# Three attentions whose score products use half the rows of the array, two heads side by side, and whose ends are rearranged

## The chip, the cores and the metric

The kernel runs on one core of a Trainium2 chip. Its time is the device time of one launch in microseconds (us). Lower is better. TensorE (PE) multiplies matrices, VectorE (DVE) and ScalarE (ACT) work on tiles and read what PE leaves in PSUM, GpSimd (POOL) works on tiles in SBUF, and SyncE (SP) issues most of the transfers. The launch works through eight batches, one pass of a loop for each, and ends with a recurrent part over all eight.

## The reference

A residual stream x of 8 batches, 512 tokens and 128 features goes through four layers. Each normalises x, takes an attention (or a memory) of the normalised rows and a feed-forward gate of them, and adds their product:

```python
xn = _layernorm(x, axis=-1)
s = _L1_attn_ref(xn, L1_attn_Wq, L1_attn_Wk, L1_attn_Wv, L1_attn_Wo)
g = _silu(_L1_ffn_ref(xn, L1_ffn_w_gate, L1_ffn_w_up, L1_ffn_w_down))
x = x + s * g
```

The attentions of the first three layers have 16 heads of 8 dimensions. The first sees all 512 keys; the other two are causal and have an output projection. All is fp32. The change touches these three attentions, and of the first layer also the end of its gate, a ternary feed-forward under a silu.

## The kernel before

Each pass of the loop holds, in order: the first attention (below: the full one), with the hidden layers of the ternary feed-forward beside it; the normalisation and projections of the second layer and its causal attention (the second), with a feed-forward and late experts beside it; a local attention; the third layer's causal attention (the third), with a gated unit and projections beside it; a second local attention, the last feed-forward and the experts.

Queries and keys are fp32. They are split into three bf16 parts each, high, middle and low, stored in DRAM and spread from there (`spread_loads`) so that rows of the contraction are pairs of a query part and a key part: 3 by 3 pairs of 8 dimensions are the 72 rows of a bf16 product. `qs` and `ks` hold 16 heads side by side in those rows, with two more rows for the maximum.

One attention works in four groups of four heads, on a grid of steps, eight to a group. `first_scores` makes queries by keys in PSUM banks 0 and 1 (line 440); in the causal attentions another product, of the identity and a mask of -1e30, adds the mask to the diagonal block (line 446). DVE reduces each bank to the negative maximum of its rows (line 618), and the product of score item n waits until item n-2 is reduced. When a group is through, PE transposes its maxima (line 468), ACT and DVE split them into two bf16 parts, and SP writes these as rows 72 and 73 of `qs` (line 566). Twelve steps after its first item, `second_scores` makes keys by queries with the 74 rows (line 458), so that the maximum is already taken off; ACT takes the exponential (line 538) from a ring of three banks; GpSimd clears above the diagonal in the causal attentions; and every second step four products of 32 columns side by side weigh the values (line 501). At a group's end the sums come back by a transpose (line 474) and DVE divides.

A full attention has 16 items of one head and one tile of queries in a group. A causal one has 11: one item with four heads for the first tile, two with two heads for the second tile, and one for each head of the others. Work of the feed-forward is called in between by step numbers (`yield`). `keep_busy` adds products that nobody reads (line 96): in the second attention they stand between the score products of the last steps. At the end of the second and third attention PE transposes `att`, ACT copies it (line 552), PE projects it (line 516), and DVE copies the result from PSUM before it goes on (line 631).

Of the kernel before, what the change touches and what calls it, by code (L numbers as in the profile page):

```python
# [26 lines left out]
E3, H3 = 8, 256  # L27
BELOW = 1.0 - 2.0 ** -22
# [291 lines left out]

def spread_loads(nc, K, engine, queries=True, keys=True):

    engine.wait_ge(K.saved, 32)
    for g in range(NG):
        heads = slice(4 * g, 4 * g + 4)
        part = lambda m: K.parts_d[m].rearrange("i (d h) t -> i d h t", d=HD)[:, :, heads, :]
        if keys:
            engine.dma_start(K.ks[72:74, heads, :], K.ones_d[:, heads, :]).then_inc(K.spread[g], 16)
        for i in range(3):
            rows = slice(24 * i, 24 * i + 24)  # L330
            if queries:
                engine.dma_start(K.qs[rows, heads, :],
                                 part(0)[i].unsqueeze(0).to_broadcast([3, HD, 4, T])).then_inc(K.spread[g], 16)
            if keys:
                engine.dma_start(K.ks[rows, heads, :], part(1)).then_inc(K.spread[g], 16)


class Beside:
# [10 lines left out]
    FILLED = {}  # L349
    started = False  # L350
# [19 lines left out]
def attention(nc, K, causal, wo=None, bo=None, combine=True, beside=None, after_store=False,  # L370
# [9 lines left out]
    QUADS, LAG, KR = 3, 12, 74  # L380
# [36 lines left out]
    with ExitStack() as tmp:  # L417
# [5 lines left out]
        with nc.Block() as block:  # L423
            @block.tensor
            def _(pe):
# [6 lines left out]
                def first_scores(n):  # L432
                    g, (t, heads) = n // PER, items[n % PER]
                    b, keys = n % 2, (t + 1) * P if causal else T
                    if n % PER == 0:
                        pe.wait_ge(K.spread[g], 7 * 16)
                    if n >= 2:
                        pe.wait_ge(reduced, n - 1)
                    for i, j in enumerate(heads):
                        mm = nc.tensor.matmul(K.ps[:, b, i * keys:(i + 1) * keys],  # L440
                                              K.qs[0:72, 4 * g + j, t * P:(t + 1) * P], K.ks[0:72, 4 * g + j, 0:keys],
                                              start=(i == 0), stop=not causal)
# [8 lines left out]
                def second_scores(m):  # L451
                    g, (k, j) = m // 16, divmod(m % 16, 4)
                    h, b = 4 * g + j, bank("second", m)
                    if m % 16 == 0:
                        pe.wait_ge(rows, 32 * (g + 1))
# [2620 lines left out]
```

## Time and profile before

| | |
|---|---|
| median of three runs | 4192.31 us (4190.34 to 4197.16) |
| the profiled execution | 4196.52 us, span 4193.1 us |
| PE busy | 3506.4 us, 84% |
| DVE busy | 2530.1 us, 60% |
| ACT busy | 1823.9 us, 43% |
| mean granted TensorE clock | 0.939 |

The span is the time from the first to the last instruction of the profiled execution. A share of busy time is an average over all stages. Matmuls are pipelined, so a product's row shows more time than it holds the array: what it costs in a stream is the distance between the starts of two rows.

### The profile page before, as it was taken

How to read it: one execution, taken by the hardware profiler on the slowest of the kernel's cores; microseconds unless marked ns; L12 is line 12 of the kernel's file. 1: busy time of each engine (PE TensorE's matmuls, PEld its weight loads, DVE VectorE, ACT ScalarE, POOL GpSimd, SP SyncE). 2: the span in 40 equal slices, each digit the busy share in tenths (PEclk: the TensorE clock that was granted, in tenths of full speed). 3: DMA queues.
4: the chain of work that ended last, by engine and by line, in shares of the span. 5: the costliest groups of instructions: out<-in, count | busy, mean ns of one | idle time of the engine just before them, and what ended most of it. 6: DMA issues, size and time to landing. Idle time of an engine off the chain costs nothing. (4 is left out here: it accounts for less than half of the span.)

```text
span 4193.1 us, 55509 instructions
## 1 busy us (share of the span) xinstructions
PE 3506.4 (84%) x19466; PEld 1814.7 (43%) x19615; DVE 2530.1 (60%) x5500; ACT 1823.9 (43%) x3753; POOL 821.5 (20%) x721
## 2 busy tenths in 40 slices
PE   3988798888988889887988889888898879888867
PEld 1444444444344444454444443444434544444434
DVE  3566655666556655666556665566556665566655
ACT  1544444444443535444444444444354444444414
POOL 1023300331012400233003310124002230033114
PEclk9999999999999999999999999999999999999978
DMA  4000111001011010000111010110200001110130
GB/s 155 25 17 26 36 30 34 31 4 61 5 34 34 1 65 25 17 26 32 34 34 31 4 63 4 34 34 1 65 28 14 27 36 30 34 31 4 63 84 21
DMA packets 87847, 140.06 MB, mean 33 GB/s; under 512 B 12472, under 2 KB 62466, under 8 KB 85002
## 3 DMA queue, kind: packets, MB, share of 16 engines
q1 hardware_dynamic: 81042, 127.30, 9.5%
q10 hardware_dynamic: 6522, 9.06, 0.7%
q8 instruction: 169, 2.77, 0.3%
q14 instruction: 114, 0.93, 0.1%
HBM read 106.14 MB, written 29.39 MB: 32 GB/s over the span
## 5 line engine op out<-in xcount | busy, mean ns | idle before, releaser
L618 DVE TENSOR_REDUCE nmax<-banks 128x1 f32<-128x512 f32 (+3 forms) x1216 | 761.1, 658 | 392.5 <-PE banks L440 228.2
L538 ACT ACTIVATE probs<-banks 128x512 f32<-128x512 f32 (+3 forms) x1024 | 475.7, 526 | 302.9 <-PE banks L458 299.9
L440 PE MATMUL banks<-ks,qs 72*128 72x512 bf16 (+3 forms) x1536 | 464.1, 348 | 98.3 <-DVE nmax L618 68.3
L458 PE MATMUL banks<-qs,ks 74*128 74x512 bf16 (+3 forms) x1536 | 461.9, 338 | 41.2 <-ACT probs L538 17.2
L96 PE MATMUL banks<-filler,identb 128*128 128x512 bf16 x1576 | 427.9, 392 | 36.0 <-PEq L76 26.5
L440 PEld LDWEIGHTS banks<-ks,qs 72*128 72x128 bf16 x1536 | 144.0, 101 | 418.4 <-DVE nmax L618 246.2
L538 ACT ACTIVATE early<-banks 128x256 f32<-128x256 f32 (+3 forms) x512 | 198.1, 440 | 196.6 <-PE banks L458 196.6
L1295 ACT ACTIVATE probs<-banks,nm 128x192 f32<-128x192 f32 x512 | 172.6, 422 | 229.9 <-DVE nm L1247 229.9
L501 PE MATMUL banks<-probs,v 128*32 128x512 f32 (+3 forms) x2048 | 239.1, 539 | 32.4 <-POOL probs L584 22.9
L253 POOL TENSOR_TENSOR rstd<-var,neghalf 128x4 f32<-128x4 f32 (+1 forms) x16 | 21.2, 1324 | 1246.2 <-DVE var L204 1137.8
L96 PEld LDWEIGHTS banks<-filler,identb 128*128 128x128 bf16 x1712 | 171.5, 101 | 205.0 <-issue 63.5
L458 PEld LDWEIGHTS banks<-qs,ks 74*128 74x128 bf16 x1536 | 142.1, 100 | 234.6 <-ACT probs L538 79.0
L1329 POOL TENSOR_TENSOR probs<-probs,inv 128x768 f32<-128x768 f32 x128 | 187.1, 1467 | 259.7 <-DVE inv L1257 259.7
L603 DVE RECIPROCAL rden<-banks 128x16 f32<-128x16 f32 x96 | 24.4, 254 | 317.9 <-PE banks L474 317.0
L446 PE MATMUL banks<-mask_q,identb 128*128 128x128 bf16 (+2 forms) x704 | 186.2, 265 | 0.0
L1199 PE MATMUL banks<-ident,probs 128*128 128x128 f32 x896 | 141.5, 295 | 49.9 <-POOL probs L1329 32.5
L1254 DVE TENSOR_REDUCE total<-probs 128x4 f32<-128x768 f32 x128 | 122.0, 953 | 84.6 <-ACT probs L1295 80.4
L584 POOL TENSOR_SCALAR_AFFINE_SELECT probs<-probs 128x512 f32<-128x512 f32 x128 | 97.3, 760 | 382.4 <-ACT probs L538 382.4
L584 POOL TENSOR_SCALAR_AFFINE_SELECT early<-early 128x512 f32<-128x512 f32 x128 | 92.8, 725 | 397.8 <-ACT early L538 397.8
L1247 DVE TENSOR_REDUCE nm<-banks 128x4 f32<-128x768 f32 x128 | 119.9, 937 | 64.1 <-PE banks L1180 63.9
L1990 PE MATMUL banks<-xnT,w_up_s 128*128 128x512 f32 x320 | 150.6, 609 | 1.4
L1199 PEld LDWEIGHTS banks<-ident,probs 128*128 128x128 f32 x896 | 101.2, 147 | 89.6 <-POOL probs L1329 47.4
(453 smaller groups left out, 6528.2 us busy)
## 6 DMA issues: line engine op xcount, KB each, us to landing
qs<-parts_scratch SPq DMA_DIRECT2D x300, 96.0 KB
ks<-parts_scratch SPq DMA_DIRECT2D x288, 96.0 KB
parts_scratch<-parts SPq DMA_DIRECT2D x50, 384.0 KB, 2.5
shared<-in_w_h SPq DMA_DIRECT2D x17, 1024.0 KB, 7.6
shared<-in_w SPq DMA_DIRECT2D x25, 256.0 KB, 4.0
qs<-max_parts SPq DMA_DIRECT2D x192, 4.0 KB
xn<-in_x SPq DMA_DIRECT2D x9, 256.0 KB, 2.7
factor_scratch<-g SPq DMA_DIRECT2D x9, 256.0 KB, 2.2
```

The source lines that it names most:

```text
L96: nc.tensor.matmul(K.ps[:, bank, :], K.identb[:, :], K.filler[:, :], start=True, stop=True)
L440: mm = nc.tensor.matmul(K.ps[:, b, i * keys:(i + 1) * keys], K.qs[0:72, 4 * g + j, t * P:(t + 1) * P], K.ks[0:72, 4 * g + j, 0:keys], star ...
L446: mm = nc.tensor.matmul(diagonal, K.identb[:, :], K.mask_q[:, :].unsqueeze(1).to_broadcast([P, n_heads, P]), start=False, stop=True)
L458: nc.tensor.matmul(K.ps[:, b, q0:T], K.ks[0:KR, h, k * P:(k + 1) * P], K.qs[0:KR, h, q0:T], start=True, stop=True).then_inc(scored2, 1)
L501: mm = nc.tensor.matmul(K.ps[32 * j:32 * j + 32, 5, q0:T], K.v32[:, k, 4 * g + j, :], probs[:, 4 * (q % QUADS) + j, q0:T], start=(k == 0), ...
L538: nc.scalar.activation(probs[:, 4 * (q % QUADS) + m % 4, q0:T], K.ps[:, bank("second", m), q0:T], ACT.Exp, scale=scale).then_inc(exped, 1)
L584: nc.gpsimd.affine_select(diagonal, diagonal, [[0, 4], [1, P]], ALU.is_ge, 0.0, base=0, channel_multiplier=-1).then_inc(masked, 1)
L618: nc.vector.tensor_reduce(nmax[:, t, h:h + len(heads)], K.ps[:, n % 2, 0:len(heads) * keys].rearrange("p (j k) -> p j k", k=keys), AX.X, A ...
L1199: mm = nc.tensor.transpose(K.ps[:, 4 + e, o:o + P], probs[:, w % RING, e, i, (k - t + 1) * P:(k - t + 2) * P], K.ident[:, :])
L1295: a = nc.scalar.activation(probs[:, w % RING, e, i, 64:256], K.ps[:, 2 * u + e, 256 * i + 64:256 * i + 256], ACT.Exp, bias=nm[:, u, e, i:i ...
L1329: nc.gpsimd.tensor_tensor(x, x, inv[:, w % 2, :, :].rearrange("p e t -> p (e t)").unsqueeze(2).to_broadcast([P, 4, SPAN]), ALU.mult).then_ ...
L1990: mm = nc.tensor.matmul(K.ps[:, 2 * (n % 2) + m, :], K.w3_up[:, e, (2 * m + c) * P:(2 * m + c + 1) * P], K.xnT[:, :], start=True, stop=True)
```

## The change

Seven pairs of parts are left of the nine (the products of the middle and the low part of the keys with the low part of the queries are left out): 56 rows, and with the maximum's two 58. These fit in half of the array's rows. Heads 0 and 1 of a group lie in partitions 0 to 63 of `qs` and `ks`, heads 2 and 3 in partitions 64 to 127, and every score product names its half by `tile_position`. The mask product, the transposes, the weighing and the extra products are made as before. In the full attention the items alternate between the halves (heads 0, 2 for each tile, then 1, 3), and the second products take the heads in the order 2, 0, 3, 1. A causal group has 12 items: the first tile's item of four heads becomes two of two.

Each group's spread is issued for each half apart: 14 transfers for 7, and the rows of the maximum 4 for 2. The silu of the first layer's gate becomes an exponential on ACT and an addition, a reciprocal and a product on DVE, at step 38 (it was at the end), and the output products of that feed-forward start at step 32 (was 36). In the second attention ACT copies the transposed `att` before the gate's silu (was after). The copy of line 631 goes: DVE reads the projection from PSUM in the operation that follows.

```diff
@@ spread_loads
-        heads = slice(4 * g, 4 * g + 4)
-            engine.dma_start(K.ks[72:74, heads, :], K.ones_d[:, heads, :]).then_inc(K.spread[g], 16)
-        for i in range(3):
-            rows = slice(24 * i, 24 * i + 24)
+        for e in range(2):
+            heads = slice(4 * g + 2 * e, 4 * g + 2 * e + 2)
+            for i, n in enumerate((3, 3, 1)):
+                rows = half_rows(2 * e, HD * n, 24 * i)
...
@@ attention
-        items = [(0, (0, 1, 2, 3)), (1, (0, 1)), (1, (2, 3))] + [(t, (j,)) for t in (2, 3) for j in range(4)]
-        by_step = (0, 1, 2, 3, 5, 6, 8, 9, 11)
+        items = [(t, pair) for t in (0, 1) for pair in ((0, 1), (2, 3))] + [(t, (j,)) for t in (2, 3) for j in (0, 2, 1, 3)]
+        by_step = (0, 2, 3, 4, 6, 7, 9, 10, 12)
     else:
-        items = [(t, (j,)) for j in range(4) for t in range(NT)]
+        items = [(t, (j,)) for pair in ((0, 2), (1, 3)) for t in range(NT) for j in pair]
...
+    HEADS, ROWS = (2, 0, 3, 1), 4 * 16
@@ first_scores
-                                              K.qs[0:72, 4 * g + j, t * P:(t + 1) * P], K.ks[0:72, 4 * g + j, 0:keys],
-                                              start=(i == 0), stop=not causal)
+                                              K.qs[rows, slot, t * P:(t + 1) * P], K.ks[rows, slot, 0:keys],
+                                              start=(i == 0), stop=not causal, tile_position=(64 * (j // 2), 0))
@@ second_scores
-                    nc.tensor.matmul(K.ps[:, b, q0:T], K.ks[0:KR, h, k * P:(k + 1) * P], K.qs[0:KR, h, q0:T],
-                                     start=True, stop=True).then_inc(scored2, 1)
+                    nc.tensor.matmul(K.ps[:, b, q0:T], K.ks[half_rows(j, KR), slot, k * P:(k + 1) * P],
+                                     K.qs[half_rows(j, KR), slot, q0:T], start=True, stop=True,
+                                     tile_position=(64 * (j // 2), 0)).then_inc(scored2, 1)
@@ sync
-                    for i in range(2):
-                        sp.dma_start(K.qs[72 + i:73 + i, 4 * g:4 * g + 4, :], mparts[:, g % 2, i, :]).then_inc(rows, 16)
+                    for e in range(2):
+                        for i in range(2):
+                            sp.dma_start(K.qs[half_rows(2 * e, 1, SCORE_ROWS + i), 2 * g:2 * g + 2, :],
+                                         mparts[2 * e:2 * e + 2, g % 2, i, :]).then_inc(rows, 16)
@@ the ends
+                o = K.att[:, :, :]
-                    ch.do(nc.vector.tensor_copy(K.att[:, :, :], o))
-                    ch.do(nc.vector.tensor_tensor(K.att[:, :, :], K.att[:, :, :], K.g[:, :, :], ALU.mult))
+                    ch.do(nc.vector.tensor_tensor(K.att[:, :, :], o, K.g[:, :, :], ALU.mult))
-        nc.scalar.activation(K.g[:, :, :], K.g[:, :, :], ACT.Silu).then_inc(self.g_ready, 1)
+        nc.scalar.activation(self.e, K.g[:, :, :], ACT.Exp, scale=-1.0).then_inc(self.e_ready, 1)
```

PE's order in the second attention, before, at the step that starts a group's items (L440 first scores, L446 mask, L458 second scores, L468 transposes of the maxima, L501 weighing):

```order
L501 MATMUL banks<-early,v 32x512 x4
L440 MATMUL banks<-ks,qs 128x128 x4
L446 MATMUL banks<-mask_q,identb 128x512
L458 MATMUL banks<-qs,ks 128x256 x2
L468 MATMUL banks<-ident,nmax 4x128 x4
L440 MATMUL banks<-ks,qs 128x256 x2
L446 MATMUL banks<-mask_q,identb 128x2x128
```

The same place after (L458 first scores, L464 mask, L476 second scores, L487 transposes, L520 weighing):

```order
L520 MATMUL banks<-early,v 32x512 x4
L458 MATMUL banks<-ks,qs 128x128 x2
L464 MATMUL banks<-mask_q,identb 128x256
L476 MATMUL banks<-qs,ks 128x256
L458 MATMUL banks<-ks,qs 128x128 x2
L464 MATMUL banks<-mask_q,identb 128x256
L476 MATMUL banks<-qs,ks 128x256
L487 MATMUL banks<-ident,nmax 4x128 x4
```

The item of four heads has become two, and a half-array product and a whole-array one (mask, transpose) now take turns.

SP's order for one group's spread, before:

```order
L328 DMA ks<-ones_scratch 2x2048
L332 DMA qs<-parts_scratch 24x1x2048
L335 DMA ks<-parts_scratch 24x2048
L332 DMA qs<-parts_scratch 24x1x2048
L335 DMA ks<-parts_scratch 24x2048
L332 DMA qs<-parts_scratch 24x1x2048
L335 DMA ks<-parts_scratch 24x2048
```

And after, for one half of a group:

```order
L342 DMA ks<-ones_scratch 2x1024
L347 DMA qs<-parts_scratch 24x1x1024
L350 DMA ks<-parts_scratch 24x1024
L347 DMA qs<-parts_scratch 24x1x1024
L350 DMA ks<-parts_scratch 24x1024
L347 DMA qs<-parts_scratch 8x1024
L350 DMA ks<-parts_scratch 8x1024
```

Each transfer carries half the columns, and there are twice as many of them.

## Rows read from the trace of the kernel before

**Rows 1.** The page, part 1: busy time, share of the span, instructions.

```profile
PE 3506.4 (84%) x19466; PEld 1814.7 (43%) x19615; DVE 2530.1 (60%) x5500; ACT 1823.9 (43%) x3753; POOL 821.5 (20%) x721
```

**Rows 2.** Part 5, costliest groups: busy, mean ns; idle before it, releaser.

```profile
L618 DVE TENSOR_REDUCE nmax<-banks 128x1 f32<-128x512 f32 (+3 forms) x1216 | 761.1, 658 | 392.5 <-PE banks L440 228.2 <-PE banks L446 151.2
L440 PE MATMUL banks<-ks,qs 72*128 72x512 bf16 (+3 forms) x1536 | 464.1, 348 | 98.3 <-DVE nmax L618 68.3 <-PEq L76 12.7 <-DMA ks<-parts_scratch 10.1
L458 PE MATMUL banks<-qs,ks 74*128 74x512 bf16 (+3 forms) x1536 | 461.9, 338 | 41.2 <-ACT probs L538 17.2 <-DVE max_parts L595 14.2 <-DMA qs<-max_parts 4.9
```

**Rows 3.** Busy time by stretch (windows): PE, weight loads, DVE, ACT, POOL; clock.

```profile
118.00:130.00 12.00, 11.49 (x60) 3.51 (x59) 10.13 (x17) 10.03 (x18) 0.00 (x0) 1.00 0.00 1
207.00:224.00 17.00, 13.87 (x69) 6.87 (x69) 13.77 (x26) 2.96 (x4) 1.27 (x1) 0.70 0.16 55
228.10:236.10 8.00, 7.51 (x66) 3.33 (x69) 5.73 (x11) 4.46 (x15) 1.93 (x4) 1.00 0.06 18
258.00:280.00 22.00, 21.35 (x156) 11.17 (x157) 1.76 (x7) 10.14 (x27) 3.82 (x6) 1.00 0.01 2
364.00:387.00 23.00, 20.10 (x108) 10.93 (x110) 15.72 (x35) 6.46 (x8) 1.02 (x1) 1.00 0.04 12
```

**Rows 4.** Timeline of PE in the local attention: start, length, instructions.

```profile
329.18 0.50 PE L1173 MATMUL banks<-mask_bands,identb 128*128 128x384 bf16 x2
329.61 0.92 PE L1180 MATMUL banks<-shared 64*128 64x192 f32 x8
```

**Rows 5.** Timeline of the full attention, part of two steps.

```profile
131.40 2.48 DVE L618 TENSOR_REDUCE nmax<-banks 128x1 f32<-128x512 f32 x4 [0.82 <-PE banks L440]
...
132.75 0.10 PEld L440 LDWEIGHTS banks<-ks,qs 72*128 72x128 bf16 x1 [0.48 <-DVE nmax L618]
132.75 0.39 PE L440 MATMUL banks<-ks,qs 72*128 72x512 bf16 x1
...
132.98 0.38 PE L458 MATMUL banks<-qs,ks 74*128 74x512 bf16 x1
...
133.29 1.06 PE L501 MATMUL banks<-probs,v 128*32 128x512 f32 x8
...
134.28 0.39 PE L440 MATMUL banks<-ks,qs 72*128 72x512 bf16 x1
```

**Rows 6.** Timeline of PE in the last steps of the second attention.

```profile
263.03 0.38 PE L96 MATMUL banks<-filler,identb 128*128 128x512 bf16 x1
263.25 0.38 PE L458 MATMUL banks<-qs,ks 74*128 74x512 bf16 x1
263.47 0.81 PE L96 MATMUL banks<-filler,identb 128*128 128x512 bf16 x3
264.21 0.43 PE L501 MATMUL banks<-early,v 128*32 128x128 f32 x8
```

**Rows 7.** Timeline of PE in the middle of the second attention.

```profile
229.17 0.40 PE L440 MATMUL banks<-ks,qs 72*128 72x128 bf16 x4
229.40 0.38 PE L446 MATMUL banks<-mask_q,identb 128*128 128x512 bf16 x1
229.62 0.38 PE L458 MATMUL banks<-qs,ks 74*128 74x256 bf16 x2
229.84 0.60 PE L468 MATMUL banks<-ident,nmax 128*4 128x128 f32 x4
```

**Rows 8.** Timelines of SP and PE: rows of the maximum, and a short transfer.

```profile
232.18 1.19 SPq L566 DMA_DIRECT2D qs<-max_parts  x2
...
234.55 0.60 PE L458 MATMUL banks<-qs,ks 74*128 74x512 bf16 x2 [0.20 <-DMA qs<-max_parts]
...
327.97 0.26 SPq L328 DMA_DIRECT2D ks<-ones_scratch  x1
```

**Rows 9.** Timeline of DVE at the ends of attentions.

```profile
174.65 0.69 DVE L638 TENSOR_TENSOR att<-att,g 128x512 f32<-128x512 f32 x1 [0.92 <-ACT g L693]
...
285.08 0.69 DVE L631 COPY att<-banks 128x512 f32<-128x512 f32 x1 [2.77 <-PE banks L516]
```

More of the change, by code:

```diff
@@ L27 @@
 E3, H3 = 8, 256
+SCORE_ROWS = 7 * HD
+SPREAD = 14 * 16
 BELOW = 1.0 - 2.0 ** -22
@@ L318, in _, with half_rows, half_slot @@
                     then[1](act)
+def half_rows(j, n, first=0):
+    return slice(64 * (j // 2) + first, 64 * (j // 2) + first + n)
+def half_slot(g, j):
+    return 2 * g + j % 2
 def spread_loads(nc, K, engine, queries=True, keys=True):
@@ L324, in spread_loads @@
     for g in range(NG):
-        heads = slice(4 * g, 4 * g + 4)
-        part = lambda m: K.parts_d[m].rearrange("i (d h) t -> i d h t", d=HD)[:, :, heads, :]
-        if keys:
-            engine.dma_start(K.ks[72:74, heads, :], K.ones_d[:, heads, :]).then_inc(K.spread[g], 16)
-        for i in range(3):
-            rows = slice(24 * i, 24 * i + 24)
-            if queries:
-                engine.dma_start(K.qs[rows, heads, :],
-                                 part(0)[i].unsqueeze(0).to_broadcast([3, HD, 4, T])).then_inc(K.spread[g], 16)
-            if keys:
-                engine.dma_start(K.ks[rows, heads, :], part(1)).then_inc(K.spread[g], 16)
+        slots = slice(2 * g, 2 * g + 2)
+        for e in range(2):
+            heads = slice(4 * g + 2 * e, 4 * g + 2 * e + 2)
+            part = lambda m: K.parts_d[m].rearrange("i (d h) t -> i d h t", d=HD)[:, :, heads, :]
+            if keys:
+                engine.dma_start(K.ks[half_rows(2 * e, 2, SCORE_ROWS), slots, :],
+                                 K.ones_d[:, slots, :]).then_inc(K.spread[g], 16)
+            for i, n in enumerate((3, 3, 1)):
+                rows = half_rows(2 * e, HD * n, 24 * i)
+                if queries:
+                    engine.dma_start(K.qs[rows, slots, :], part(0)[i].unsqueeze(0).to_broadcast([n, HD, 2, T])
+                                     ).then_inc(K.spread[g], 16)
+                if keys:
+                    engine.dma_start(K.ks[rows, slots, :], part(1)[0:n]).then_inc(K.spread[g], 16)
 class Beside:
@@ L349 @@
     FILLED = {}
+    TURNED_FIRST = 1 << 18
     started = False
@@ L435, in first_scores @@
                     if n % PER == 0:
-                        pe.wait_ge(K.spread[g], 7 * 16)
+                        pe.wait_ge(K.spread[g], SPREAD)
                     if n >= 2:
@@ L527, in _ @@
                         if g >= 2:
-                            act.wait_ge(rows, 32 * (g - 1))
+                            act.wait_ge(rows, ROWS * (g - 1))
                         nc.scalar.activation(mparts[:, g % 2, 0, :], K.ps[0:4, bank("maxima", g), :],
@@ L537, in _ @@
                         q0 = k * P if causal else 0
-                        nc.scalar.activation(probs[:, 4 * (q % QUADS) + m % 4, q0:T], K.ps[:, bank("second", m), q0:T],
+                        nc.scalar.activation(probs[:, 4 * (q % QUADS) + HEADS[m % 4], q0:T],
+                                             K.ps[:, bank("second", m), q0:T],
                                              ACT.Exp, scale=scale).then_inc(exped, 1)
@@ L547, in _ @@
                     beside.run(beside.on_scalar, s)
-                beside.run(beside.on_scalar)
+                beside.run(beside.on_scalar, beside.TURNED_FIRST)
                 if wo is not None:
@@ L552, in _ @@
                     nc.scalar.activation(oT[:, 0, :], K.ps[:, 0, :], ACT.Identity).then_inc(attT_ready, 1)
+                beside.run(beside.on_scalar)
             @block.sync
@@ L2110, in _ @@
                 for g in range(NG):
-                    sp.wait_ge(K.spread[g], 7 * 16)
+                    sp.wait_ge(K.spread[g], SPREAD)
         K.clear()
@@ L2337, in batch_loop @@
         K.clear()
-    K.qs, K.ks = sb("qs", [P, H, T], BF16), sb("ks", [P, H, T], BF16)
+    K.qs, K.ks = sb("qs", [P, 2 * NG, T], BF16), sb("ks", [P, 2 * NG, T], BF16)
     K.qT, K.kT, K.v_tm = K.late_qT, K.late_kT, K.late_v
```

29 lines of the change are left out of this document (19 added, 10 removed).

## Prediction, written before the changed kernel was run

> **What bounds the kernel now.** I read the page first. PE is busy 84% of the span, DVE 60%, ACT 43% [rows 1]; of the groups, DVE's maxima and the two kinds of score products stand on top, and the reader is to see that the first products wait mostly for DVE and DVE for the first products: a loop between two engines, not one full engine [rows 2]. The chain of waits shows nothing here, since it follows only the last part of the launch. So I took the busy times by stretch. In the full attention PE holds 11.49 of 12 us and DVE 10.13; in the middle of the second attention PE holds 7.51 of 8 and DVE 5.73; in its last steps PE holds 21.35 of 22 while DVE has 1.76 [rows 3]. PE is the tight engine in the causal attentions, at the end wholly. Then I read timelines for what one product costs in a stream. A bf16 product of 512 columns holds PE 0.22 us (263.03 to 263.25) [rows 6].
>
> **The price of the new thing.** No score product shares the array before. The local attention does it, though: eight fp32 products of 64 rows, in pairs in the two halves, take 0.92 us, and each of the four pairs goes as one, since in series eight times 192 columns of fp32 (512 take 0.45 us, from the weighing's two sets of four in 0.99 us less a switch [rows 5]) would be 1.35. So the halves do work at once [rows 4]. The same rows show what it costs to come there. Two bf16 products of 384 columns stream in 0.33 us, but the half-array products start 0.43 us after them: 0.10 lost. From three extra products (3 x 0.216) to the weighing it is 0.74 us: 0.09 lost [rows 6]. From a score product to the weighing 0.31 instead of 0.22 [rows 5]. Every change of the array's shape costs 0.09 to 0.10 us; I take 0.10, which includes a weight load no longer hidden for its first 10 ns. Bounds: 0.09, and 0.15 where fp32 weights follow.
>
> The Trainium skill says this too, in TensorEngine Tiling (Array Packing), Key Properties: changing the tiling mode drains the engine. By that rule, the trace agrees. Its table of Theoretical Speedup promises up to two times for contractions of at most 64 rows; by that alone every two score products that stand side by side would cost one, and the change would be a gain. That is rival (1), whose price is from rows.
>
> How often the shape changes, I counted in PE's order from the first score product to the last weighing. Full attention: 29 before, 71 after. Second: 31 and 174. Third: 31 and 158. That is 312 more in a pass, 31 us of PE in each of 8 passes if none is hidden. The reason stands in the order: in the causal attentions a mask product of the whole array follows every item, and a second product comes behind it.
>
> **Full attention, per pass.** First twelve steps: the two items of a step overlap (-0.22), and come between fp32 products of the whole array (+0.10 and +0.15): +0.03 a step, +0.4. Middle, 20 steps: in two steps the loop is weighing (0.99 us with its switches), first product, three reductions in turn, the last first product (released by DVE), the last second product, weighing [rows 5]. Now the last second product runs beside the first one: -0.22 per two steps, ten times, -2.2. Last twelve steps: a second product waits for a bank of ACT's ring, nothing gained, 0. End: the silu is gone from the way (DVE waits 0.92 us for it; its product could start at 173.73 instead of 174.65 [rows 9]), but the extra products at the end hold PE until about 175.5, so -0.5. Its exponential and DVE's three operations lie at step 38, where DVE has little to do. Sum -2.3.
>
> **Second attention.** First twelve steps: 18 items with 36 changes, 3.6 us; PE holds 13.87 of 17 and waits for DVE [rows 3], which hides half: +1.7. Middle: per group of eight steps 12 items give 24 changes, the two sets of transposes 4 more, 2.8 us; second products of one step that now stand together overlap, 0.22 + 0.16 + 0.11 + 0.06, and at two seams 0.11 each: -0.8. Waits of PE there are small (one is the 0.20 for the rows [rows 8]); products follow each other without a hole, 0.22 us apart, from 229.17 to 229.84 [rows 7]. I let them take 0.6. 1.4 for each of two and a half groups: +3.5. Last steps: 22 second products with an extra product behind each, 44 changes less the 6 that stand at a weighing anyway: 38 x 0.10 = +3.8, on an engine without a hole. End: without the copy DVE could start its product at 285.08, but the silu with its table load now comes behind ACT's copy and ends near 285.5: -0.2.
>
> **Third attention.** The same front, with 20.10 of 23 us busy: +2.0. Middle +3.5. Last twelve steps: no extra products, pairs overlap (-1.6), 21 more changes around the projections' products (+2.1), half of it in waits: 0. End: the copy of 0.69 us goes, -0.7.
>
> **Rows of the maximum.** Two issues take 1.19 us on SP, the last one's landing releases the second product 1.18 us later [rows 8]. Four of the twelve group starts in a pass stand at this minimum (three in the second attention, one in the third). Four transfers of two heads instead of two of four: between 0.26 us each (the short transfer of ones) and the 0.57 of today, so -0.1 to +1.2 us at such a start. It is nearest to today's own row, +1.2; the three steps between transposes and second products become some 0.2 us longer each and take 0.6 of it: 4 x 0.6 = +2.4. The spread's issues, 14 for 7 in a group, lengthen from 16 to about 28 us on SP. In front of the second attention they are done just before SP is wanted for the first rows of maxima; in front of the others a local attention or the experts are longer. 0, with up to +2 if one is late.
>
> Sum per pass: -2.3 + (1.7 + 3.5 + 3.8 - 0.2) + (2.0 + 3.5 + 0 - 0.7) + 2.4 = +13.7 us, eight times 110 us. The profiled execution took 4196.5 us (span 4193.1, 3.4 around it), so 4306; the median of the runs lies 4.2 lower, 4302. I say 4300.
>
> **Rivals.** (1) The change of shape is free between bf16 products, the measured ones have fp32 on one side. Then only overlap is left: full attention -2.6 - 2.2 - 0.5, second -2.0 - 0.2, third -2.0 - 1.6 - 0.7, in all -11.8 us a pass: 4098. For it: no pair of bf16 neighbours of two shapes is in the trace. Against: the loss is the same 0.09 to 0.10 with bf16 before and with bf16 behind [rows 4, 5]. Faster on balance as soon as a change costs under some 0.045 us. Chance 0.08. (2) Changes cost 0.10, but the waits of the loops take all of them but those in the last steps of the second attention: -2.3 + 3.6 - 0.7 = +0.6 a pass, 4197. For it: first products do wait for DVE, 68.3 us [rows 2]. Against: PE at 7.51 of 8. Chance 0.12. (3) The rows of the maximum and the spread decide: each of twelve group starts 1.2 us later instead of 2.4 us in all, +26 a pass, 4398. Chance 0.10. (4) The halves don't overlap in these products, as two heads in one item share a half: no -2.2 and -2.6 in the full attention and no -0.8 and -1.6 behind, +22 a pass, 4370. Against: [rows 4]. Chance 0.08.
>
> **Numbers.** My forecast (slower by 1 to 4%) has 0.62. Below it, 4210 has fronts and middles at half their price (+3 a pass); above, 4370 holds rival 4 and changes at 0.15. Range 4210 to 4370; (1), most of (2) and (3) lie outside. 0.2% is about what a measurement of this kernel tells from none. Faster: (1) 0.08 and of (2) 0.05, 0.13. Same: 0.05, of (2). Slower: the rest, 0.82.
>
> **What would show it.** In the trace after: pairs of score products with starts under 0.02 us apart in the full attention, and its two-step period at 3.09 instead of 3.31 us; from first product to mask 0.10 us more than its columns; in the last steps of the second attention 0.32 us between starts where 0.22 was; L566's successor with four issues over 1.2 to 2.4 us. Wrong, if the causal attentions keep their length, or if the granted clock falls in stretches where it was full: half-array products may load the array less, and no row of before shows that.

## The result, and the profile after

The changed kernel takes 4545.28 us (median of four runs, 4540.88 to 4555.44) against 4193.54: a ratio of 1.0841, interval 1.0826 to 1.0856. That is 352 us slower, or 44 us in each of the eight passes. I had forecast 4300, slower by 110 us, 13.7 a pass. The direction was right; the size is three times what I wrote and far above my range (4210 to 4370).

The page of the kernel after, part 1, and of part 5 the groups that answer to [rows 1, 2]:

```profile
PE 3830.7 (84%) x19546; PEld 1783.1 (39%) x19695; DVE 2573.0 (57%) x5572; ACT 1842.5 (41%) x3753; POOL 819.3 (18%) x721
...
L641 DVE TENSOR_REDUCE nmax<-banks 128x1 f32<-128x512 f32 (+3 forms) x1280 | 776.2, 634 | 579.7 <-PE banks L464 325.0
...
L458 PE MATMUL banks<-ks,qs 56*128 56x512 bf16 (+3 forms) x1536 | 488.5, 377 | 95.2 <-DVE nmax L641 61.1
L476 PE MATMUL banks<-qs,ks 58*128 58x512 bf16 (+3 forms) x1536 | 446.4, 376 | 52.0 <-ACT probs L557 20.1
```

PE's share of busy time is 84% as before, of a longer span; shares hide such a change. What moved is the idle time ahead of DVE's maxima, from 392.5 to 579.7 us: DVE waits longer for the products, now mostly for the mask product (L464). And the mean granted clock of TensorE is 0.880, before 0.939. Added up over the record of the clock, it was at its lower level, 1.2 of 2.4 GHz, for 1091 us, before for 516. That is the largest difference between the two traces, and the prediction had only named it as a way to be wrong. (A low clock over a whole launch is given below by this record, which runs 2 to 4 us past the span.)

What I expected of single products came out. In the full attention, two products in different halves start together (timeline after; L458 first, L476 second scores, L520 weighing):

```profile
660.25 0.39 PE L458 MATMUL banks<-ks,qs 56*128 56x512 bf16 x1
...
661.42 0.39 PE L458 MATMUL banks<-ks,qs 56*128 56x512 bf16 x1 [0.17 <-DVE nmax L641]
661.42 0.39 PE L476 MATMUL banks<-qs,ks 58*128 58x512 bf16 x1
...
662.36 1.07 PE L520 MATMUL banks<-probs,v 128*32 128x512 f32 x8
663.35 0.39 PE L458 MATMUL banks<-ks,qs 56*128 56x512 bf16 x1
```

Two steps take 3.10 us (660.25 to 663.35) where they took 3.31; I had said 3.09. In the second attention a product of 512 columns is followed by the mask product 0.31 us later, and that of 128 columns (0.05 us) by the next score product after 0.16:

```profile
770.49 0.38 PE L458 MATMUL banks<-ks,qs 56*128 56x512 bf16 x1
...
770.80 0.23 PE L464 MATMUL banks<-mask_q,identb 128*128 128x128 bf16 x1
...
770.96 0.33 PE L476 MATMUL banks<-qs,ks 58*128 58x384 bf16 x1
```

So a change of shape costs 0.10 us between two bf16 products as well, and rival (1) falls. The Trainium skill puts it as a drain at each change (TensorEngine Tiling (Array Packing), Key Properties), without a figure there; by that, the trace agrees, at 0.09 to 0.11 us each.

The spread is not a cause: in front of the second attention's pass shown above SP issues its last transfer of it at 756.6 and is wanted for the rows of the maximum at 764.1 only, and no first product of the trace waits for a spread transfer.

Two things that the prediction's sum did not have stand in the same trace. First, the gate's end in the full attention (timeline of DVE, ACT and PE):

```profile
691.80 0.64 ACT L717 ACTIVATE hid_b<-g 128x512 f32<-128x512 f32 x1
...
692.47 0.43 DVE L728 TENSOR_SCALAR hid_b<-hid_b 128x512 f32<-128x512 f32 x1 [3.91 <-ACT hid_b L717]
692.93 3.35 DVE L729 RECIPROCAL hid_b<-hid_b 128x512 f32<-128x512 f32 x1
696.32 0.69 DVE L731 TENSOR_TENSOR g<-g,hid_b 128x512 f32<-128x512 f32 x1
696.93 0.25 DVE L626 RECIPROCAL rden<-banks 128x16 f32<-128x16 f32 x1
697.22 0.48 DVE L628 TENSOR_TENSOR att<-banks,rden 128x32 f32<-128x32 f32 x4
697.85 1.93 PE L520 MATMUL banks<-probs,v 128*32 128x512 f32 x8 [5.87 <-DVE att L628]
699.71 1.03 PE L476 MATMUL banks<-qs,ks 58*128 58x512 bf16 x3
```

The reciprocal of 512 columns takes 3.35 us, eight times the addition in front of it (0.43). The Trainium skill (VectorE: DVE Perf Modes, First, the fixed hardware budget) has the reciprocal as an iterative divide with a repeat count of 8; by that, the trace agrees, at 7.8 times the addition. Behind it in DVE's queue stands the division of the group's sums, and the next weighing may not overwrite their bank before that. PE stands 5.87 us, and then works at the lower clock: the weighing at 697.85 shows 1.93 us for what took 1.07.

Second, the clock. The first sixteen second products of the second attention, as stretches in pass 2 and in pass 3 of the same execution (columns as in [rows 3]):

```profile
768.26:780.05 11.79, 10.75 (x73) 3.95 (x73) 8.19 (x14) 6.72 (x17) 2.54 (x4) 1.00 0.00 1
1297.82:1314.55 16.73, 16.73 (x73) 4.34 (x73) 7.82 (x13) 7.14 (x17) 2.54 (x4) 0.50 0.01 1
```

The same 73 products take 11.79 us at full clock and 16.73 at half. That is 4.94 us for 16.7 us of low clock, 0.30 for each. In other stages that a trace shows at both levels it is more, up to 0.44 (rows_in_four and tail_switches below). Before the change this stage took 9.60 to 9.64 us in every pass, at full clock.

By stage, mean over the passes, with the microseconds of low clock in brackets, from the starts of the score products in both traces:

| | first score to first second score | second scores 1-16 | 17-32 | 33-48 | 49-64 |
|---|---|---|---|---|---|
| full attention, before | 35.3 (2.7) | 13.0 | 13.5 | 12.0 | 12.3 |
| after | 36.1 (3.0) | 13.6 (2.6) | 12.7 | 14.4 | 17.0 (10.2) |
| second, before | 17.2 (9.4) | 9.6 | 13.0 (0.2) | 13.9 (6.6) | 13.7 |
| after | 22.9 (18.1) | 14.3 (8.4) | 18.6 (12.3) | 15.8 (9.4) | 16.7 |
| third, before | 23.1 | 13.8 | 16.2 (5.1) | 14.9 (1.3) | 14.0 (1.3) |
| after | 25.6 | 19.6 (9.8) | 20.5 (13.2) | 14.9 (0.4) | 13.6 |

### The profile page after: what moved, and what is told of

It reads as the page before. It is cut to its first block and busy times, and to the rows that moved or that the text cites. A ratio compares the mean times of both kernels' runs of the same rounds, so it can differ in the third digit from the quotient of the medians.

```text
span 4543.3 us, 56641 instructions
## 1 busy us (share of the span) xinstructions
PE 3830.7 (84%) x19546; PEld 1783.1 (39%) x19695; DVE 2573.0 (57%) x5572; ACT 1842.5 (41%) x3753; POOL 819.3 (18%) x721
## 5 line engine op out<-in xcount | busy, mean ns | idle before, releaser
L641 DVE TENSOR_REDUCE nmax<-banks 128x1 f32<-128x512 f32 (+3 forms) x1280 | 776.2, 634 | 579.7 <-PE banks L464 325.0
L458 PE MATMUL banks<-ks,qs 56*128 56x512 bf16 (+3 forms) x1536 | 488.5, 377 | 95.2 <-DVE nmax L641 61.1
L476 PE MATMUL banks<-qs,ks 58*128 58x512 bf16 (+3 forms) x1536 | 446.4, 376 | 52.0 <-ACT probs L557 20.1
L98 PE MATMUL banks<-filler,identb 128*128 128x512 bf16 x1592 | 454.5, 403 | 31.0 <-PEq L78 19.5
L520 PE MATMUL banks<-probs,v 128*32 128x512 f32 (+3 forms) x2048 | 279.1, 626 | 73.4 <-DVE att L628 46.9
L557 ACT ACTIVATE early<-banks 128x256 f32<-128x256 f32 (+3 forms) x512 | 209.3, 437 | 303.3 <-PE banks L476 301.2
L458 PEld LDWEIGHTS banks<-ks,qs 56*128 56x128 bf16 x1536 | 120.7, 97 | 519.2 <-DVE nmax L641 292.6
L476 PEld LDWEIGHTS banks<-qs,ks 58*128 58x128 bf16 x1536 | 111.7, 95 | 283.8 <-ACT probs L557 98.9
L464 PE MATMUL banks<-mask_q,identb 128*128 128x128 bf16 (+1 forms) x768 | 215.6, 281 | 0.0
L464 PEld LDWEIGHTS banks<-mask_q,identb 128*128 128x128 bf16 x768 | 76.5, 100 | 224.7 <-issue 217.7
```

The source lines that it names most:

```text
L98: nc.tensor.matmul(K.ps[:, bank, :], K.identb[:, :], K.filler[:, :], start=True, stop=True)
L458: mm = nc.tensor.matmul(K.ps[:, b, i * keys:(i + 1) * keys], K.qs[rows, slot, t * P:(t + 1) * P], K.ks[rows, slot, 0:keys], start=(i == 0) ...
L464: mm = nc.tensor.matmul(diagonal, K.identb[:, :], K.mask_q[:, :].unsqueeze(1).to_broadcast([P, n_heads, P]), start=False, stop=True)
L476: nc.tensor.matmul(K.ps[:, b, q0:T], K.ks[half_rows(j, KR), slot, k * P:(k + 1) * P], K.qs[half_rows(j, KR), slot, q0:T], start=True, stop ...
L520: mm = nc.tensor.matmul(K.ps[32 * j:32 * j + 32, 5, q0:T], K.v32[:, k, 4 * g + j, :], probs[:, 4 * (q % QUADS) + j, q0:T], start=(k == 0), ...
L557: nc.scalar.activation(probs[:, 4 * (q % QUADS) + HEADS[m % 4], q0:T], K.ps[:, bank("second", m), q0:T], ACT.Exp, scale=scale).then_inc(ex ...
```

## Experiments

**Parts of the change undone.** My theory after the trace was that the gate costs some 60 us, the causal attentions nearly all the rest, and the half-array form in the full attention nothing either way. gate_back puts the gate's end back:

```diff
-    OUT_STEP, GATE_STEP = 32, 38
+    OUT_STEP = 36
-        yield self.GATE_STEP
+        yield 1 << 19
         act.wait_ge(self.g_in, 1)
-        nc.scalar.activation(self.e, K.g[:, :, :], ACT.Exp, scale=-1.0).then_inc(self.e_ready, 1)
+        nc.scalar.activation(K.g[:, :, :], K.g[:, :, :], ACT.Silu).then_inc(self.g_ready, 1)
```

> The changed kernel with the gate's end of before: output products from step 36, silu on ACT at the very end, no exponential, addition, reciprocal and product. Theory A (the reciprocal of 128x512 holds DVE 3.35 us at step 38, the group's division queues behind it and PE stands 5.87 us): the last sixteen second products of the full attention fall from 17.05 to about 12.3 us and the third sixteen from 14.4 to 12.0, in all 7 to 9 us a pass less the silu's wait that comes back (0.5): 4545 - 8 x 7.5 = 4485. Rival B (the half-array products and the fallen clock lengthen the full attention, the gate hardly matters): 4535 to 4545.

Measured: 4483.0 us (4461.9 to 4494.0), ratio to the kernel before 1.0699 (1.0658 to 1.0740). Theory A: the last sixteen second products of the full attention are back at 12.36 us. gate_alone is the reverse, the kernel before with only the new gate and the earlier output products:

> The kernel before with the changed gate alone: output products from step 32, at step 38 an exponential on ACT and an addition, a reciprocal and a product on DVE. Theory A (the reciprocal blocks the division): +7 to +8 us a pass, 4193 + 60 = 4253. The prediction's own step said nothing lost and 0.5 us won: 4189. Rival: the stall is covered where the halves are not in use: 4200.

Measured: 4273.6, ratio 1.0205 (1.0172 to 1.0238), 81 us. The gate costs 62 us as part of the change and 81 alone, and my step had it as a small gain. full_only keeps the half-array form in the full attention only (the key of HALVES is whether an attention is causal), and ends_only nowhere:

```diff
+HALVES = {False: True, True: False}
+    halves = HALVES[causal]
+    at = lambda j: (64 * (j // 2), 0) if halves else None
```

> As gate_back, but the half-array form only in the full attention; both causal attentions have their 9 products, 74 rows, 11 items a group, 7 transfers and 2 row transfers of before. Theory A (nearly all of the rest is the causal attentions: changes of the array's shape, fallen clock, rows of the maximum): 4485 less 8 x 36 = about 4195, granted clock back at 0.93. Rival B (half is in the full attention's halves): 4330.

Measured: 4198.4, ratio 1.0016 (1.0004 to 1.0028), clock 0.941. The causal attentions in halves cost 285 us, 36 a pass.

> As full_only, but the full attention too as before: what is left of the change is the copy taken away at the ends of the second and third attention and ACT's copy of the transposed att ahead of the silu. Prediction's step: 0.9 us a pass less, 4193 - 7 = 4186. If the halves gain in the full attention 2.2 us a pass as the prediction had it, full_only is 14 us or more below this kernel; by the stages of the changed kernel's trace (first group +0.9, second -0.8, before them +0.7) it is level with it within 8 us.

Measured: 4194.1, ratio 1.0010 (1.0000 to 1.0020). The ends' edits bring nothing that can be measured, where I had 7 us. Halves in the full attention are level (4 us over ends_only): its second group of second products falls from 13.47 to 12.79 us (-0.68, where the sum has -0.88), and the third rises from 12.03 to 12.63. That rise is the rows of the maximum: with two transfers (below) the third group takes 12.28, and in combined, with the high parts' issued first, 12.01.

**The price of a change of shape by itself.** tail_switches is the kernel before with another form of its extra products between the second scores at the second attention's end:

```diff
-                                keep_busy(nc, K, 0, 1)
+                                nc.tensor.matmul(K.ps[:, 0, :], K.identb[0:64, :], K.filler[0:64, :], start=True,
+                                                 stop=True, tile_position=(0, 0))
```

> The kernel before, with one edit: the extra products between the second scores of the second attention's last steps use 64 of the array's rows (the columns stay 512), so the array changes its shape 40 times more in a pass and nothing else moves. Theory A (a change of shape costs 0.10 us on an engine without a hole): the last sixteen second products take 13.7 + about 3 us, the pass 4.0 us more, 4193 + 32 = 4225, granted clock unchanged there. Rival B (changes between bf16 products are free): 4193. Rival C (the half-array products also take the clock down here): above 4250.

Measured: 4251.2 (4236.6 to 4275.7), ratio 1.0128 (1.0105 to 1.0150), 58 us. The last sixteen second products, as stretches in pass 2 and pass 3, and before the change:

```profile
765.05:790.08 25.03, 24.54 (x99) 9.39 (x98) 0.74 (x5) 8.77 (x19) 1.91 (x3) 0.63 0.00 1
1269.17:1286.21 17.04, 16.72 (x100) 7.52 (x98) 0.74 (x5) 8.51 (x19) 1.91 (x3) 1.00 0.00 1
```

```profile
745.10:758.80 13.70, 13.55 (x95) 8.00 (x98) 0.74 (x5) 7.86 (x18) 1.91 (x3) 1.00 0.00 0
```

At full clock 17.04 against 13.70, and 0.6 more in the sixteen before: 3.9 us for 40 changes, 0.10 each, 31 us a launch. That is theory A. In three of eight passes of the profiled execution, the slowest of the four, the clock falls in this stretch, for 18 us each time, and takes 8 us more (0.44 for each microsecond): so something of what rival C names is there too, and the launch's 4251 is at its bound.

What brings that low clock isn't shown. Not the short stops alone: in the kernel after, the same stretch has nearly as many changes, and is at full clock in all eight passes, and so it is in gate_back, halves_rows_in_two, halves_filled and no_mask, at 16.67 us every time:

```profile
816.35:833.02 16.67, 16.16 (x95) 7.83 (x98) 0.74 (x5) 8.59 (x19) 1.90 (x3) 1.00 0.00 1
```

And not the half-array products alone: half_tail, next, makes both the scores and the extra products between them in halves, and has no low clock there. The Trainium skill describes a like case (TensorE: Matmul & The Clock Gate, A second HAM failure mode: psum-queue depth-cycling): frequent short idle times between groups of products make the clock go up and down. Three of eight passes here are in keeping with that; the stretch at 16.67 us, in five kernels, is not.

half_tail takes the other way, from gate_back: the scores of that stretch are in halves already, and the extra products join them.

> gate_back (4483) with the extra products between the second scores of the second attention's last steps in 64 rows, as the scores there: 22 changes of shape fewer in a pass. Theory A (0.10 us each, PE without a hole, the clock full there): the last sixteen second products go from 16.67 to between 14 and 15.0 us, 4483 - 18 = 4465. Rival B (half-array products take the clock down when the whole-array ones go from between them): low clock appears in a stretch where gate_back has none, 4483 or more.

Measured: 4503.5 (4483.3 to 4544.7), ratio 1.0745 (1.0694 to 1.0795). The stage itself goes as theory A says, 16.67 to 13.97 us, 0.12 for each of 22 changes, with no low clock in it, so rival B falls. But the launch is no faster (the two intervals overlap, so it isn't shown slower either): from the third attention's start to the next pass this trace, of the slowest of its four runs (4544.7), has 57 us of low clock a pass, gate_back's 36 (means of the first seven passes). Why the clock falls there more often, these runs don't settle.

**The mask product.** In halves it is a change of shape behind every item, so I left it out in both forms. In both the maximum is taken without the mask, and the rest is as it is.

```diff
-                                              start=(i == 0), stop=not causal, ...
-                    if causal:
-                        mm = nc.tensor.matmul(diagonal, K.identb[:, :], ...
+                                              start=(i == 0), stop=(i == len(heads) - 1), ...
```

> gate_back without the product that adds the mask in the causal attentions (the maximum is then taken over all keys of a tile's width; the rest is as it is). Read against the next kernel: with the mask the half-array form in the causal attentions cost 285 us (4483 against 4198) at 270 more changes of shape a pass; without it there are 126 more. Theory A (changes of shape and the clock that falls with them): the difference shrinks to about half, 110 to 150 us, 4150 + 130 = 4280. Rival B (half-array products themselves, or their transfers, cost it or take the clock down): the difference stays over 220 us, 4400.

> full_only (half-array form in the full attention alone) without the mask product. The mask products are 2048 columns a group, 0.85 us of PE, 6.8 us a pass; most of it lies on PE's path: 4198 less about 45 = 4153.

Measured: no_mask 4328.6 (ratio 1.0327, 1.0293 to 1.0361), no_mask_whole 4179.5 (0.9977, 0.9965 to 0.9990). The difference between the forms falls from 285 to 149 us, at 126 changes more a pass where there were 270. Both levels lie above what I wrote (4280 and 4153); the difference is what was asked, and it goes nearly in proportion to the changes (1.05 and 1.18 us a launch for each change a pass, 0.13 and 0.15 a change): theory A. Both differences hold the rows' transfers and the twelfth item of a group too. What these two are worth can be bounded: 144 changes make 136 us of the difference, 0.118 each with the clock that falls with them; at that price 270 changes make 255 of the 285, and 30 us are left for all that doesn't go with the changes, an estimate. The rows alone account for that (below), so the twelfth item costs little.

The levels say something too. The mask products are some 55 us of PE's columns (6.8 us a pass, by the expectation above). Without them the kernel with half-array causal attentions gains 154 us, nearly what they and 144 changes at 0.10 come to (170). The whole-array form gains 19, a third of the 55: there PE's time isn't given back in full. Still, no_mask_whole is the fastest kernel here, 13 us under the kernel before. What it leaves out is the mask under the maximum, which may then come from a key that is masked later.

**Rows of the maximum.** rows_in_four is the kernel before with four transfers:

```diff
-                    for i in range(2):
-                        sp.dma_start(K.qs[72 + i:73 + i, 4 * g:4 * g + 4, :], mparts[:, g % 2, i, :]).then_inc(rows, 16)
+                    for e in range(2):
+                        for i in range(2):
+                            sp.dma_start(K.qs[72 + i:73 + i, 4 * g + 2 * e:4 * g + 2 * e + 2, :],
+                                         mparts[2 * e:2 * e + 2, g % 2, i, :]).then_inc(rows, 16)
```

> The kernel before, with the rows of the maximum written by four transfers of two heads each for two of four heads. Prediction's step: four of twelve group starts in a pass 0.6 us later, 2.4 us a pass, 4193 + 19 = 4212. Rival B (every group start pays the whole 1.19 us): 4193 + 114 = 4307. Rival C (hidden everywhere): 4193.

Measured: 4274.7, ratio 1.0181 (1.0164 to 1.0198): 82 us where I had 19. SP's row of this kernel, four issues, against 1.19 us for two in [rows 8]:

```profile
408.05 2.38 SPq L567 DMA_DIRECT2D qs<-max_parts  x4
```

An issue of this transfer takes 0.60 us with two heads as with four. At full clock the second attention's first group of second products goes from 9.61 to 10.73 us, and the way to the first second score of the third from 23.1 to 24.2: these starts pay the 1.1 us whole. So does, nearly, one that I hadn't counted, the full attention's third group (12.03 to 12.91), while its first two pay nothing (13.00 and 13.47 as before). And the third attention's first group now meets low clock in five of eight passes of the profiled execution (the slowest of six): 19.1 us where it takes 13.84, 0.39 us for each microsecond of low clock. rows_filled feeds PE in that wait:

```diff
+                    bank_read("second", m)
                     if m % 16 == 0:
+                        keep_busy(nc, K, b, 5)
                         pe.wait_ge(rows, 64 * (g + 1))
-                    bank_read("second", m)
```

> rows_in_four (4275, 82 us over the kernel before), with five extra products of 512 columns put on PE directly ahead of each group's wait for the rows of the maximum. The array form is never changed, so this asks whether the clock's fall comes from PE standing. Theory A (the longer waits bring the low clock: the third attention's first group has 13.4 us of it in five of eight passes, and only there takes 19.1 instead of 13.8 us): with PE fed in the waits that low stretch goes, 8.4 us of low clock a pass and some 3.3 us of time, 4275 - 26 = 4250; the extra products cost nothing where the wait is 1.1 us and longer. Rival B (the clock falls for another reason): 4275 or more.

Measured: 4256.8, ratio 1.0147 (1.0133 to 1.0162), 18 us below rows_in_four (14 by the two ratios). The group in pass 3 of rows_in_four, and the same in rows_filled:

```profile
1392.90:1411.98 19.08, 18.61 (x91) 9.96 (x92) 9.15 (x16) 8.26 (x20) 1.90 (x3) 0.65 0.00 1
```

```profile
1382.63:1397.55 14.92, 13.46 (x97) 7.42 (x98) 10.07 (x18) 7.91 (x20) 2.55 (x4) 1.00 0.01 2
```

More products, and 4.2 us less: the clock stays at its full level in all eight passes. Against a pass at full clock (13.84) the five products cost 1.1 us. Over the launch the low level falls from 624 to 388 us. Neither kernel has a half-array score product or a change of shape that the kernel before lacks, so theory A is shown: PE's standing in the waits brings the low clock there.

halves_rows_in_two gives gate_back two transfers, each writing a row in both halves:

```diff
+                    for i in range(2):
+                        sp.dma_start(K.qs[SCORE_ROWS + i:SCORE_ROWS + i + 65:64, 2 * g:2 * g + 2, :],
+                                     mparts[:, g % 2, i, :]).then_inc(rows, 16)
```

> gate_back (4483) with two transfers for the rows of the maximum: each writes one part's rows in both halves (partitions 56 and 120, and 57 and 121). Theory A (the rows' issues cost here what they cost in rows_in_four, 82 us, and an issue of two partitions takes the 0.6 us of one): 4483 - 80 = 4400. Rival B (in the half-array form other waits cover them): 4483. Rival C (the issue doubles with the two partitions): 4483.

Measured: 4437.4, ratio 1.0584 (1.0558 to 1.0611): 46 us back, between A and B. Some 12 to 18 us of that lie in the full attention (123.4 us up to the next attention, where full_only takes 125.0 and gate_back 125.6). Rival C falls: two issues in a row take 1.07 to 1.12 us here, and the full attention gains (its first group takes 12.24 us where gate_back's takes 12.52 without low clock). halves_filled adds the five extra products to its causal waits:

> halves_rows_in_two (4437) with five extra products of the whole array ahead of each causal group's wait for the rows of the maximum. Theory A (a large part of what is left over the whole-array form is low clock that begins in waits: 61 us of it a pass in the second attention against 21): the low clock there falls by 20 us a pass or more, worth 0.3 us each, while the extra products cost up to 1 us in the starts that wait less than that: 4437 - 35 = 4400. Rival B (it begins in the many short stops at changes of shape, which no filling of waits removes): the low clock stays, 4440 to 4480.

Measured: 4396.1, ratio 1.0491 (1.0472 to 1.0511), 41 us below. The low level falls from 818 to 525 us over the launch, about what the kernel before has (516), and the second attention's first group from 15.99 us (14.6 low) to 12.08 (0.7 low). Theory A.

The extra products have a price here. The second attention's first two groups, in the first pass, at full clock in both, are lengthened by 1.08 us each (halves_rows_in_two, then halves_filled):

```profile
236.69:247.51 10.82, 10.68 (x74) 3.95 (x74) 7.62 (x13) 6.72 (x17) 2.40 (x4) 1.00 0.00 1
247.51:261.87 14.36, 12.47 (x90) 4.79 (x89) 10.64 (x22) 7.32 (x18) 2.69 (x5) 1.00 0.08 21
```

```profile
235.99:247.90 11.91, 11.72 (x79) 4.26 (x79) 7.60 (x13) 6.71 (x17) 2.54 (x4) 1.00 0.03 8
247.90:263.34 15.44, 13.43 (x94) 5.08 (x94) 11.06 (x22) 7.31 (x18) 2.54 (x4) 1.00 0.05 14
```

In the third attention three stages get 1.1 to 1.2 us longer at full clock, and the last group 1.2 shorter (12.45, where gate_back's passes at full clock take 13.64). That is 4.3 us a pass, and 6 to 7 with the stages that can be compared only at about equal low clock: 34 to 54 us a launch. So the low clock that went was worth 41 us and this, 75 to 95. It also says what is no matter of the clock: with the low clock of the kernel before, the causal attentions in halves are still far slower than as a whole array (198 us over full_only, the extra products included).

**Towards a faster version.** hi_first edits only SP's order in the kernel before:

```diff
-                    sp.wait_ge(hi_ready, g + 1)
-                    sp.wait_ge(lo_ready, g + 1)
                     for i in range(2):
+                        sp.wait_ge((hi_ready, lo_ready)[i], g + 1)
```

> The kernel before, with one edit on SyncE: the transfer of the high parts is issued when they are ready and not after the low parts too, so its 0.57 us lie beside DVE's operation on the low parts. rows_in_four showed that seven group starts in a pass pay every delay of the rows in full. Theory A (four of them stand at the minimum today and would each win 0.57 us, 2.3 us a pass, and some low clock may go with it): 4193 - 18 = 4175, down to 4150. Rival B (another wait is right behind): 4190.

Measured: 4188.2, ratio 0.9982 (0.9968 to 0.9996), 7 us faster and at the edge of what can be told. Three starts gain (17.2 to 16.55, 23.1 to 22.55, 9.61 to 9.26), some 1.5 us a pass, a part of it clock, where I had 2.3; a part is given back behind.

> Half-array form in the full attention alone, the rows of the maximum in two transfers in every attention and the high parts' issued first, the gate as before, the ends as changed. By stages of the runs so far: full attention 1.4 us a pass less (halves_rows_in_two), causal fronts and first groups 2.0 less (hi_first): 4193 - 27 = 4166 if the clock leaves it, 4180 if it eats half, as in hi_first.

> combined with two extra products ahead of each causal group's wait for the rows. Theory A (they keep the clock up in the third attention's middle, 10 us of low clock a pass, 3 us): 10 to 20 us under combined. Rival B (no wait is left there to hide them, 0.43 us at each of eight starts): 20 us over it.

Measured: combined 4220.8 (1.0069, 1.0052 to 1.0086), combined_fed 4214.0 (1.0053, 1.0036 to 1.0070). Both are slower than the kernel before, against my expectation, and the fed one is 7 us under the other, less than theory A's 10 to 20. Gains of the starts are in combined's trace (third attention's 22.55, second's first group 9.26; the second's own start stays at 17.3), but its full attention has 8.8 us of low clock a pass where full_only has 2.9, and takes 126.8 us for 125.0 up to the next attention. Of the versions that keep the mask, none beats the kernel before by more than hi_first does. What moves the clock's low stretches into the full attention in combined stays open.

## Why the prediction was wrong

**Right:** the direction; the price of a change of shape (0.10 predicted, 0.10 measured in tail_switches); that halves run together (rival 4 falls: 3.10 us for two steps); that the causal attentions pay and the full one doesn't; the second attention's last steps, +2.96 us in the last sixteen second products without any low clock, where I had 3.8 for twenty-two.

**Step 1, the largest part of the 352 us: "Waits of PE there are small ... I let them take 0.6", "waits for DVE, which hides half".** The causal attentions got 270 changes of shape more. Charged in full they are 27 us a pass; I took off 5.6 for overlap and some 7 for waits, and charged 14.5. halves_filled, which has nearly the low clock of the kernel before and two row transfers, leaves 198 us to full_only. Less its extra products (34 to 54 us), and with the 12 us that its full attention gains by the two transfers, about 155 to 175 us or 19 to 22 a pass are left for the changes of shape. That is the full price less the overlap (21.4): little or nothing was hidden. This is an estimate by subtraction, and the proportion in the two kernels without the mask supports it. I had the reason on the page and didn't use it: products wait for DVE and DVE for the products [rows 2]. My reading, which no run isolates: in a loop of two engines PE's wait is no reserve, since a product that is 0.1 us late makes the maximum late, and that the product after the next. DVE's idle time before the maxima, up 187 us, is in keeping with that, though the low clock and the gate are in it too.

**Step 2, the largest miss: the clock, which the sum didn't have at all.** The closing paragraph named it, and the sum and the range had no term. Feeding the waits of the causal attentions took away low clock worth 75 to 95 us, so that much was avoidable by that alone. It is not all: the launch has 575 us more at the low level than before, and at 0.30 to 0.44 us for each that is an estimated 170 to 250 us, a good part of it in the other terms, as the gate's.

**Step 3: "Its exponential and DVE's three operations lie at step 38, where DVE has little to do": -0.5 a pass, measured +7.8 (62 us).** An idle engine isn't a free one if something behind the new work has a date. I took the operations for three like the others and didn't look for a reciprocal's price; the nearest row had 16 columns (0.25 us), and 512 are 32 times as many, which bounds it between 0.25 and 8 us. Measured: 3.35.

**Step 4: the rows of the maximum, +2.4 a pass.** The issue was sized rightly (0.57 a transfer was "nearest to today's own row", 0.60 measured), but "Four of the twelve group starts" and "take 0.6 of it" were wrong: 10 us a pass alone, low clock included, 5.8 in the change. A start that isn't at its minimum today can get there as soon as the minimum rises, as the full attention's third group did.

**Step 5: the full attention without its gate, -1.8 a pass, measured +0.5** (full_only over ends_only, with four row transfers; about -1.0 without their 1.5); and the ends, -0.9, measured +0.2.

Together: 110 forecast; gate +66 (62 for -4), rows +27 (46 for 19), changes of shape +50 (about 166 for 116), clock +85, full attention without its rows +6, ends +9: 353, where 352 was measured. These terms overlap in the clock, which most runs move, so each is good to some 20 us, and that they add up is by construction: each is a difference between two runs of one chain, and the last one, of feeding the waits and what is left, is divided between the clock and the changes of shape by the price of the extra products.

Of the rivals, (2) is refuted by all of this. (3) was nearer than my sum on what the rows cost (14.4 us a pass for my 2.4, 10 measured alone), but they decide nothing: they are 46 of 352 us, and the spread costs nothing that the trace shows. The +22 a pass of (4) isn't what its terms add up to (20.9 with each overlap taken once, 24.1 with the -0.8 for each of five groups), which changes nothing.

## What to carry to other kernels

Count changes of the array's shape before counting rows saved: at 0.10 us each one change costs as much as half the product of 512 columns that two halves can save, so halves pay only where several such products stand in a row. Where two engines wait for each other in turn, charge every delay in full until a run shows a part of it hidden; but don't count time taken away as won (the mask product's 55 us gave 19 in the whole-array form). And where a change adds waits on PE, add a term for the lower clock from stretches that the trace shows at both levels, here 0.30 to 0.44 us for each microsecond at the lower one.

## What the runs showed of the hardware

- A DVE reciprocal of 128x512 in fp32 takes 3.35 us in all eight passes of the kernel after, an addition with a constant of the same size 0.43.
- The issue of the maximum's rows on SP takes 0.60 us with four heads or with two to one partition, and 0.54 to 0.56 where it writes to two partitions, so splitting costs by the piece.
- A stretch of the second attention with forty more changes of shape met the lower clock in three of eight passes of tail_switches; without them, and with nearly as many of them in five other kernels, it met none. What decides stays open.
- A microsecond at the lower clock cost 0.30 us in one stage, 0.39 in another and 0.44 in a third.
- Extra products in a wait can be worth more than they cost: 236 us less at the low level and 18 us less time in rows_filled. At full clock five of them cost 1.1 us in a start.
- A faster stage doesn't make a faster launch here: half_tail took 2.7 us a pass out of a stage without low clock, and its launch didn't become faster; combined took 1.0 us a pass out of two starts and 0.6 out of the full attention's third group, and its launch was 22 us slower than full_only.
